# The place of GpSimd's shift in the combining of a Mamba and expert layer: behind the addition of the next group but one

## The chip, the cores and the metric

The kernel runs on one core of a Trainium2 chip. The metric is the time of one execution on the device, in microseconds; the median of three runs of the kernel before is 914.01 us.

## The reference

The input is 8 sequences of 1024 tokens of 128 numbers. A first block (a Mamba-2 mixer and a small MLP) gives x1. A second block routes each of the 8192 tokens to 2 of 8 experts (with a capacity), and adds the two gated results of a token to y. The last step, which is what the change touches, is a layer norm of y without weights and a residual:

```python
m = jnp.mean(x, axis=-1, keepdims=True)
v = jnp.var(x, axis=-1, keepdims=True)
return (x - m) / jnp.sqrt(v + eps)
...
x = x + _layernorm(_L0_ffn_ref(_layernorm(x, axis=-1), L0_ffn_Wr, ...), axis=-1)
```

All of it is float32.

## The kernel before, in words

The program goes through stages with a barrier of all engines between them. In the last one GpSimd gathers token rows for each expert by indirect DMA (L1809), TensorE runs the two matrix products, and GpSimd scatters the gated results into a DRAM buffer, `choice_rows` (L1817), which has one half for the first and one for the other expert of each token.

Then comes the combining. Its 64 tiles of 128 tokens are cut into 19 groups: 14 of four tiles, then groups of 2, 2, 2, 1 and 1 (L1717). For each group:

- SP loads both halves, `ys` and `yb` (L1792, L1793; a load of four tiles is 256 KB), and stores the result (L1797). The store of group n stands in its queue behind the loads of group n+8.
- GpSimd adds the halves: `both`, L1825, one tensor_tensor over 128x512.
- VectorE takes the statistics of each tile: `moments`, L1940, then `combined`, L1946, which makes mean and variance.
- ScalarE takes the root of the variance: `rooted`, L1899.
- VectorE makes the reciprocal: `inverse`, L1951.
- GpSimd negates the mean (`minus_mean`, L1829) and multiplies it with the reciprocal (`shift`, L1834), both over 128x4.
- ScalarE applies scale and shift to each tile: `normal`, L1905.
- VectorE adds x1: `add_x1`, L1955.

All of this lies in SBUF; in the trace `ys`, `yb` and `x1` all bear the name arena, the shift is c_shift, the reciprocal c_rs, the root c_sd, mean and variance c_mv.

Each engine runs its program in the order that `in_turn` (L1743) unrolls from a list of pairs of lag and step: in its round i an engine does, for each pair in the order of the list, the step of group i - lag. The lists are:

```python
in_turn(GROUPS, [(0, load), (8, store)])                                        # SP, L1798
in_turn(GROUPS, [(0, both), (1, minus_mean), (1, shift)])                       # GpSimd, L1835
in_turn(GROUPS, [(0, rooted), (1, normal)])                                     # ScalarE, L1907
in_turn(GROUPS, [(0, moments), (1, inverse), (0, combined), (2, add_x1)])       # VectorE, L1956
```

An engine does its instructions strictly in this order; `need(engine, semaphore, n)` waits until the step of group n that raises the semaphore is done. So on VectorE the reciprocal of group n comes behind the statistics of group n+1. The values that a group's small steps pass on (`c_mv`, `c_rs`, `c_sd`, `c_sh`, `c_nm`) have places of their own for every group; only the raw statistics, `c_st`, have two places in turn.

Of the kernel before, what the change touches and what calls it, by code (L numbers as in the profile page):

```python
# [58 lines left out]
def need(eng, sem, t, back=0):  # L59

    value = t + 1 - back
    if not isinstance(value, int) or value > 0:
        eng.wait_ge(sem, value)
# [33 lines left out]
def build(nc, x, ln_w, ln_b, in_proj_w, conv_w, conv_b, dt_bias, A_log, D_skip, rms_w, out_proj_w,  # L97
# [4 lines left out]
    with ExitStack() as ctx:  # L102
# [449 lines left out]
        with ExitStack() as st:  # L552
# [47 lines left out]
            def staged(stages):  # L600

                for i in range(PAIRS + max(lag for lag, _ in stages)):
                    for lag, stage in stages:
                        if 0 <= i - lag < PAIRS:
                            stage(i - lag)
# [475 lines left out]
        with ExitStack() as st:  # L1081
            st.callback(stage_over)
            NB, G = 4, 2
            GROUPS, N = TILES // G, G * P
# [602 lines left out]
        with ExitStack() as st:  # L1687
# [30 lines left out]
            GROUPS = len(widths)  # L1718
# [17 lines left out]
            def of_group(g):  # L1736
                return slice(first_tile[g], first_tile[g + 1])
# [5 lines left out]
            def in_turn(steps, stages):  # L1743

                for i in range(steps + max(lag for lag, _ in stages)):
                    for lag, stage in stages:
                        if 0 <= i - lag < steps:
                            stage(i - lag)
# [52 lines left out]
            @block.gpsimd  # L1801
            def _(g):
                def fetch(n):
                    need(g, s_pt, n, RING)
                    need(g, s_g1, n, RING)
                    need(g, s_g2, n, RING)
                    for i in range(sizes[n]):
                        c = starts[n] + i
                        g.indirect_dma_start(xg[:, n % RING, i, :], None, table,  # L1809
                                             bass.IndirectOffsetOnAxis(ap=token_of[:, c:c + 1], axis=0),  # L1810
                                             bounds_check=TOKENS - 1, oob_is_err=False).then_inc(s_xg[n % RING], 16)

                def leave(n):
                    need(g, s_yo, n)
                    for i in range(sizes[n]):
                        c = starts[n] + i
                        g.indirect_dma_start(choice, bass.IndirectOffsetOnAxis(ap=choice_of[:, c:c + 1], axis=0),  # L1817
                                             yo[:, n % RING, i, :], None, bounds_check=2 * TOKENS - 1,
                                             oob_is_err=False).then_inc(s_scat[n % RING], 16)
                g.wait_ge(filled, 16 * FILLS)  # L1820
                staged([(0, fetch), (LAG, leave)])

                def both(n):
                    g.wait_ge(s_in[n], 32)
                    g.tensor_tensor(ys[:, of_group(n)], ys[:, of_group(n)], yb[:, of_group(n)], ALU.add).then_inc(s_ys2, 1)  # L1825

                def minus_mean(n):
                    need(g, s_var, n)
                    g.tensor_scalar(c_nm[:, n, 0:widths[n]], c_mv[:, n, 0:widths[n], 0], -1.0, None, ALU.mult).then_inc(s_nm, 1)  # L1829

                def shift(n):
                    need(g, s_nm, n)
                    need(g, s_rs, n)
                    g.tensor_tensor(c_sh[:, n, 0:widths[n]], c_nm[:, n, 0:widths[n]], c_rs[:, n, 0:widths[n]], ALU.mult).then_inc(s_sh, 1)  # L1834
                in_turn(GROUPS, [(0, both), (1, minus_mean), (1, shift)])  # L1835

            @block.tensor
            def _(pe):
# [142 lines left out]
```

## Time and profile before

| | |
|---|---|
| median of 3 runs | 914.01 us (913.89 to 914.7) |
| the profiled execution | 914.42 us, its span 912.7 us |
| GpSimd busy over the span | 474.8 us (52%) |
| VectorE busy over the span | 602.5 us (66%) |
| ScalarE busy over the span | 493.2 us (54%) |
| TensorE matmuls busy over the span | 675.3 us (74%) |
| the combining's first load is issued at | 847.96 us |
| its first addition starts at | 851.52 us |
| the last addition of x1 starts at | 904.28 us |

The span runs from the first to the last instruction of the profiled execution; all times inside it count from its start. The whole program has stages with different limits, and the shares of the span say little of the last one; TensorE does nothing in the combining.

### The profile page before, as it was taken

How to read it: one execution, taken by the hardware profiler on the slowest of the kernel's cores; microseconds unless marked ns; L12 is line 12 of the kernel's file. 1: busy time of each engine (PE TensorE's matmuls, PEld its weight loads, DVE VectorE, ACT ScalarE, POOL GpSimd, SP SyncE). 2: the span in 40 equal slices, each digit the busy share in tenths (PEclk: the TensorE clock that was granted, in tenths of full speed). 3: DMA queues.
4: the chain of work that ended last, by engine and by line, in shares of the span. 5: the costliest groups of instructions: out<-in, count | busy, mean ns of one | idle time of the engine just before them, and what ended most of it. 6: DMA issues, size and time to landing. Idle time of an engine off the chain costs nothing. (4 is left out here: it accounts for less than half of the span.)

```text
span 912.7 us, 14173 instructions
## 1 busy us (share of the span) xinstructions
PE 675.3 (74%) x3646; PEld 480.7 (53%) x3646; DVE 602.5 (66%) x2110; ACT 493.2 (54%) x1207; POOL 474.8 (52%) x631
## 2 busy tenths in 40 slices
PE   7556999999999997999999702163896777976000
PEld 3224677777777775789999501132553444543000
DVE  7755999999999983799999687795221111111354
ACT  4764566666666665788886225252442333333254
POOL 7502576676667664234443230002677777776564
PEclk9876999999999998999999655555999999899555
DMA  8930000000000001500000021002222222211862
GB/s 212 394 115 1 1 1 1 1 1 2 1 1 2 1 1 42 144 1 2 2 0 1 1 113 76 0 0 62 45 74 74 72 74 71 74 50 42 280 202 78
DMA packets 50406, 52.84 MB, mean 58 GB/s; under 512 B 7576, under 2 KB 39624, under 8 KB 50080
## 3 DMA queue, kind: packets, MB, share of 16 engines
q1 hardware_dynamic: 44496, 41.62, 14.1%
q0 software_dynamic: 5120, 10.37, 4.3%
q8 instruction: 28, 0.46, 0.2%
q14 instruction: 42, 0.34, 0.1%
q10 hardware_dynamic: 720, 0.05, 0.1%
HBM read 28.04 MB, written 24.18 MB: 57 GB/s over the span
## 5 line engine op out<-in xcount | busy, mean ns | idle before, releaser
L836 DVE SCALAR_TENSOR_TENSOR s_cv<-s_pU,tap_w,s_cv 128x256 f32<-128x256 f32 x384 | 159.6, 477 | 20.0 <-ACT s_cv L769 19.5
L1809 POOL DMA_INDIRECT arena<-token_rows,token_of x80 | 81.1, 1014 | 118.3 <-issue 118.0
L1817 POOL DMA_INDIRECT choice_rows<-arena,choice_of x80 | 79.6, 995 | 31.1 <-issue 22.9
L1932 DVE TENSOR_TENSOR arena<-e_pB,e_gate 128x384 f32<-128x384 f32 (+2 forms) x24 | 14.5, 602 | 121.6 <-PE e_pB L1868 121.6
L1883 ACT ACTIVATE e_h<-e_pH,e_bcols 128x384 f32<-128x384 f32 (+2 forms) x96 | 58.6, 616 | 63.8 <-PE e_pH L1852 61.1
L642 POOL TENSOR_TENSOR s_xa<-s_xt,arena 128x512 f32<-128x512 f32 x32 | 34.4, 1075 | 103.1 <-ACT s_xt L787 103.1
L674 PE MATMUL s_pU<-arena,w_in 128*128 128x262 f32 x256 | 72.6, 408 | 11.5 <-DVE s_cv L836 8.1
L769 ACT ACTIVATE s_cv<-s_pU,tap_b,tap_w 128x256 f32<-128x256 f32 x128 | 65.7, 560 | 27.6 <-PE s_pU L674 27.0
L1852 PE MATMUL e_pH<-e_xgT,e_w 128*128 128x384 f32 (+2 forms) x192 | 79.0, 559 | 0.0
L1860 PE MATMUL e_pO<-e_h,e_w 128*128 128x384 f32 (+2 forms) x192 | 72.7, 522 | 0.4 <-ACT e_oT L1890 0.4
L1315 PE MATMUL m_pM<-w_m,m_h 128*128 128x128 f32 x512 | 62.5, 275 | 0.0
L1306 PE MATMUL m_pH<-m_hT,w_m 128*128 128x256 f32 x256 | 60.7, 380 | 2.1 <-ACT m_h L1189 1.5
L1315 PEld LDWEIGHTS m_pM<-w_m,m_h 128*128 128x128 f32 x512 | 59.7, 192 | 0.2 <-issue 0.2
L674 PEld LDWEIGHTS s_pU<-arena,w_in 128*128 128x128 f32 x256 | 45.4, 199 | 20.8 <-DVE s_cv L836 11.0
L1150 POOL TENSOR_TENSOR arena<-arena,m_un 128x256 f32<-128x256 f32 (+1 forms) x32 | 22.4, 701 | 64.9 <-DVE m_un L1225 64.9
L1860 PEld LDWEIGHTS e_pO<-e_h,e_w 128*128 128x128 f32 x192 | 36.5, 191 | 33.1 <-issue 20.3
L1852 PEld LDWEIGHTS e_pH<-e_xgT,e_w 128*128 128x128 f32 x192 | 38.2, 210 | 27.0 <-issue 18.8
L1306 PEld LDWEIGHTS m_pH<-m_hT,w_m 128*128 128x128 f32 x256 | 46.2, 190 | 7.5 <-ACT m_hT L1182 2.6
L1189 ACT ACTIVATE m_h<-m_pH,b_col 128x256 f32<-128x256 f32 x128 | 50.1, 484 | 0.0
L1924 DVE COPY e_xgT<-e_pT 128x384 f32<-128x384 f32 (+2 forms) x24 | 14.4, 599 | 48.6 <-PE e_pT L1843 48.6
L787 ACT ACTIVATE s_xt<-s_pTr 128x512 f32<-128x512 f32 x32 | 19.1, 597 | 47.7 <-PE s_pTr L684 47.7
L1890 ACT ACTIVATE e_oT<-e_pO,e_bcols 128x384 f32<-128x384 f32 (+2 forms) x24 | 14.8, 616 | 54.9 <-PE e_pO L1860 54.9
(289 smaller groups left out, 1873.8 us busy)
## 6 DMA issues: line engine op xcount, KB each, us to landing
choice_rows<-zrow SPq DMA_DIRECT2D x16, 512.0 KB, 6.9
arena<-choice_rows SPq DMA_DIRECT2D x28, 256.0 KB, 5.1
token_rows<-arena SPq DMA_DIRECT2D x8, 520.0 KB, 5.8
n_x<-in_L_attn_x_dram SPq DMA_DIRECT2D x8, 512.0 KB, 7.6
arena<-in_L_attn_x_dram SPq DMA_DIRECT2D x8, 512.0 KB, 4.7
e_w<-in_L_ffn_W_dram SPq DMA_DIRECT2D x16, 256.0 KB, 3.2
out_dram<-arena SPq DMA_DIRECT2D x14, 256.0 KB, 2.5
decay_rows<-arena SPq DMA_DIRECT2D x2, 1024.0 KB, 4.7
```

The costliest lines, as they stand in the source:

```text
L642: g.tensor_tensor(heads(xa[:, p % 3, :]), heads(xt[:, p % 2, :]), spread(pre, p), ALU.mult).then_inc(s_xa, 1)
L674: pe.matmul(pU[m % 2][:, 0:G2 * XBLK], w_in[:, P * m:P * (m + 1)], xT[:, G2 * p:G2 * (p + 1), :].rearrange("p t c -> p (t c)"), start=True ...
L769: a.activation(by_tile(cv[:, p % 2, m, :]), columns(m)[:, :, 0:P], ACT.Identity, bias=tap_b[:, m:m + 1], scale=tap_w[:, m, 0:1]).then_inc( ...
L836: v.scalar_tensor_tensor(out=by_tile(cv[:, p % 2, m, :]), in0=columns(m)[:, :, tap:tap + P], scalar=tap_w[:, m, tap:tap + 1], in1=by_tile( ...
L1189: ins = a.activation(h1[:, m % NB, c, :], pH[half_][:, N * (c % 2):N * (c % 2 + 1)], ACT.Relu, bias=b1_col[:, c:c + 1])
L1306: ins = pe.matmul(pH[half_][:, N * c:N * (c + 1)], w_m1[:, P * f:P * (f + 1)], hT[:, m % NB, :], start=True, stop=True)
L1315: ins = pe.matmul(pM[m % 2][:, P * i:P * (i + 1)], h1[:, m % NB, c, P * i:P * (i + 1)], w_m2[:, c, :], start=(c == 0), stop=(c == NF - 1))
L1809: g.indirect_dma_start(xg[:, n % RING, i, :], None, table, bass.IndirectOffsetOnAxis(ap=token_of[:, c:c + 1], axis=0), bounds_check=TOKENS ...
L1817: g.indirect_dma_start(choice, bass.IndirectOffsetOnAxis(ap=choice_of[:, c:c + 1], axis=0), yo[:, n % RING, i, :], None, bounds_check=2 * ...
L1852: pe.matmul(pH[c][:, 0:w], we1[:, expert(n) % 2, P * c:P * (c + 1)], xgT[:, n % 3, 0:w], start=True, stop=True).then_inc(s_ph, 1)
L1860: ins = pe.matmul(pO[:, 0:w], we2[:, expert(n) % 2, c, :], hb[:, n % 2, c, 0:w], start=(c == 0), stop=(c == NF - 1))
L1883: a.activation(hb[:, n % 2, c, 0:w], pH[c][:, 0:w], ACT.Silu, bias=bcols[:, f:f + 1]).then_inc(s_h, 1)
```

## The change

GpSimd's list gives the two small steps a lag of 2 in place of 1: in round i, behind the addition of group i, it makes the negated mean and the shift of group i - 2. The other engines' lists stay as they are.

```diff
-                in_turn(GROUPS, [(0, both), (1, minus_mean), (1, shift)])
+                in_turn(GROUPS, [(0, both), (2, minus_mean), (2, shift)])
```

At the start of the combining, in GpSimd's row (L1817 scatters the last results of the experts, L1825 is the addition):

```order
 L1809 DMA arena<-token_rows,token_of 128x130 x2
 L1817 DMA choice_rows<-arena,choice_of 16384x128 x20
-L1825 TENSOR_TENSOR arena<-arena 128x512 x2
-L1829 TENSOR_SCALAR c_minus<-c_mv 128x4
-L1834 TENSOR_TENSOR c_shift<-c_minus,c_rs 128x4
-L1825 TENSOR_TENSOR arena<-arena 128x512
+L1825 TENSOR_TENSOR arena<-arena 128x512 x3
 L1829 TENSOR_SCALAR c_minus<-c_mv 128x4
 L1834 TENSOR_TENSOR c_shift<-c_minus,c_rs 128x4
```

Three additions stand ahead of the first shift where there were two; from there on one addition and one pair follow each other as before, but the pair is that of a group earlier. At the end of GpSimd's row, where the groups are small:

```order
 L1834 TENSOR_TENSOR c_shift<-c_minus,c_rs 128x2
 L1825 TENSOR_TENSOR arena<-arena 128x128
+L1829 TENSOR_SCALAR c_minus<-c_mv 128x2
+L1834 TENSOR_TENSOR c_shift<-c_minus,c_rs 128x2
 L1829 TENSOR_SCALAR c_minus<-c_mv 128x1
 L1834 TENSOR_TENSOR c_shift<-c_minus,c_rs 128x1
```

The pair of the last group of two tiles used to come directly behind the addition of the first group of one tile; now it comes behind the last addition, and two pairs of one tile follow it. The rows of TensorE, VectorE, ScalarE and SP are the same.

## Rows read from the trace of the kernel before

**Rows 1.** The page: busy tenths of GpSimd and the DMA engines, 40 slices.

```profile
POOL 7502576676667664234443230002677777776564
...
DMA  8930000000000001500000021002222222211862
```

**Rows 2.** The chain of waits around 870 us (start us, us, what).

```profile
869.12 1.70 POOL arena L1825
...
870.91 0.87 DVE c_stats L1940 x4
...
872.01 0.20 POOL c_shift L1834
```

**Rows 3.** Timeline of GpSimd (start us, us, engine, line, operation, idle before).

```profile
854.65 1.26 POOL L1825 TENSOR_TENSOR arena<-arena 128x512 f32<-128x512 f32 x1 [1.88 <-DMA arena<-choice_rows]
855.88 0.23 POOL L1829 TENSOR_SCALAR c_minus<-c_mv 128x4 f32<-128x4 f32 x1
857.05 0.20 POOL L1834 TENSOR_TENSOR c_shift<-c_minus,c_rs 128x4 f32<-128x4 f32 x1 [0.94 <-DVE c_rs L1951]
857.20 1.26 POOL L1825 TENSOR_TENSOR arena<-arena 128x512 f32<-128x512 f32 x1
...
869.08 1.74 POOL L1825 TENSOR_TENSOR arena<-arena 128x512 f32<-128x512 f32 x1
870.78 0.21 POOL L1829 TENSOR_SCALAR c_minus<-c_mv 128x4 f32<-128x4 f32 x1
...
893.62 0.20 POOL L1834 TENSOR_TENSOR c_shift<-c_minus,c_rs 128x4 f32<-128x4 f32 x1 [1.02 <-DVE c_rs L1951]
...
903.22 0.20 POOL L1829 TENSOR_SCALAR c_minus<-c_mv 128x1 f32<-128x1 f32 x1
903.53 0.19 POOL L1834 TENSOR_TENSOR c_shift<-c_minus,c_rs 128x1 f32<-128x1 f32 x1
```

**Rows 4.** Timeline of VectorE, one round.

```profile
870.91 0.87 DVE L1940 BATCH_NORM_STATS2 c_stats<-arena 128x6 f32<-128x128 f32 x4 [1.22 <-POOL arena L1825]
871.70 0.16 DVE L1951 RECIPROCAL c_rs<-c_sd 128x4 f32<-128x4 f32 x1
...
872.12 0.66 DVE L1955 TENSOR_TENSOR arena<-arena 128x512 f32<-128x512 f32 x1
```

**Rows 5.** Waits, 855 to 904, then 893.5 to 904 us (us, times, longest).

```profile
POOL c_shift L1834 <- DVE c_rs L1951: 16.0, 18, 1.0
...
POOL c_shift L1834 <- DVE c_rs L1951: 3.9, 6, 1.0
```

**Rows 6.** Timelines of VectorE and GpSimd where their additions meet.

```profile
898.18 1.19 DVE L1955 TENSOR_TENSOR arena<-arena 128x512 f32<-128x512 f32 x1 [0.17 <-ACT arena L1905]
899.30 0.47 DVE L1940 BATCH_NORM_STATS2 c_stats<-arena 128x6 f32<-128x128 f32 x2
...
898.10 0.72 POOL L1825 TENSOR_TENSOR arena<-arena 128x256 f32<-128x256 f32 x1
...
9.65 1.47 POOL L295 TENSOR_TENSOR n_hn<-n_hc,n_scale 128x768 f32<-128x768 f32 x1 [0.15 <-DVE n_scale L488]
...
10.06 1.08 DVE L493 SCALAR_TENSOR_TENSOR n_shift<-moments,n_scale 128x8 f32<-128x8 f32 x1
```

**Rows 7.** Timeline of ScalarE, one round.

```profile
872.44 1.63 ACT L1905 ACTIVATE arena<-arena,c_shift,c_rs 128x128 f32<-128x128 f32 x4
```

**Rows 8.** Busy by stretch: PE, PEld, DVE, ACT, POOL, PEclk, DMA share, GB/s.

```profile
894.00:904.00 10.00, 0.00 (x0) 0.00 (x0) 6.75 (x29) 7.93 (x22) 6.69 (x17) 0.50 0.34 106
858.00:863.00 5.00, 0.00 (x0) 0.00 (x0) 3.21 (x20) 2.96 (x9) 2.97 (x7) 0.50 1.05 391
```

**Rows 9.** Timeline of SP's queue, and DMA issues of 846 to 913 us.

```profile
860.88 0.51 SPq L1792 DMA_DIRECT2D arena<-choice_rows  x1
...
arena<-choice_rows SPq DMA_DIRECT2D x28, 256.0 KB, 5.1
```

**Rows 10.** Timeline of VectorE, its last addition.

```profile
904.28 0.29 DVE L1955 TENSOR_TENSOR arena<-arena 128x128 f32<-128x128 f32 x1 [0.17 <-ACT arena L1905]
```

## The prediction

> **What bounds the kernel now.** The page's slices come first: in the last two and a half of the 40 (from about 850 us) GpSimd is busy for four to seven tenths, so it isn't full, and the DMA share is at its height only at the start of that stretch [rows 1]. The change lies there alone. The chain of waits of that stretch says what sets its pace: it goes round in a ring of addition (L1825, GpSimd), statistics (L1940, VectorE), shift (L1834, GpSimd), and again the addition [rows 2]. The ring's times, from the rows: an addition starts at 869.08, the statistics of its group at 870.91 (1.83 later), the reciprocal (L1951) behind them at 871.70 (0.79), the shift at 872.01 (0.31) [rows 2 to 4], and the next addition 0.15 after a shift (857.05 to 857.20) [rows 3]. Together 3.08 us a group. Nothing in it has to be a ring: the reciprocal belongs to group n, but VectorE reaches it only behind the statistics of group n+1, which want the addition of n+1; and the addition of n+2 stands on GpSimd behind the shift of n. GpSimd idles for it 16.0 us in 18 waits, always for L1951 [rows 5]. From the first shift (857.05) to the thirteenth (893.62) there are twelve such rounds, 36.57 us, 3.05 each [rows 3].
>
> The addition itself is priced in two ways: the second took 1.26 us, the seventh 1.74 [rows 3]. Ahead of the second VectorE had no addition of x1 (L1955) to make yet; in the even rounds one starts 0.42 after the reciprocal, at 872.12, some 0.04 before GpSimd's [rows 2 to 4]. The reverse is there too: where GpSimd's addition began first (898.10), VectorE's at 898.18 took 1.19 in place of 0.66 [rows 4, 6]. At the start of the program a VectorE operation on 8 columns took 1.08 us; it began 0.41 us into a 1.47 us multiplication on GpSimd and ended with it [rows 6]. So of two such operations the later one waits for the earlier to be over, and doesn't merely run slower.
>
> Here a rule of the Trainium skill differs: "Advanced Engine Details and Errata", section on VectorE's performance modes, names as the conflict with GpSimd only VectorE instructions in a two-port mode, and its table gives tensor_tensor no such mode. By that alone VectorE's addition would delay nobody, and the time would be that of the lower end of the first rival; the trace disagrees (1.19 against 0.66 us).
>
> **The change, part by part.** No instruction, DMA, buffer or semaphore is added or removed. Only GpSimd's row changes: each pair of L1829 and L1834 goes behind one more addition. SP's queue, VectorE's, ScalarE's rows are as before.
>
> 1. The ring goes. The addition of n+2 is no longer behind the shift of n, whose reciprocal by then has mostly been made. GpSimd alone would need 1.23 us (854.65 to 855.88) for the addition, 0.31 from L1829 to its L1834 (903.22 to 903.53) and 0.15 to the next: 1.69; with a wait of 0.48 (1.74 less 1.26) for VectorE's addition it is 2.17 a group [rows 3].
>
> 2. What is late next. The shift of n now comes behind the addition of n+2, so ScalarE's L1905 of group n comes then, and VectorE's L1955 of n (unchanged, behind the statistics of n+2) has to wait for it, and the statistics of n+3 stand behind that. This is a ring over two groups: shift of n to its L1905 0.43 (872.01 to 872.44), four activations 1.63 [rows 7], L1955 0.59 (1.12 from its start at 898.18 to the next instruction, less the 0.53 that it waited [rows 6]), statistics of n+3 0.79, reciprocal of n+2 to shift of n+2 0.31 [rows 2, 4]. Sum 3.75, or 1.88 a group. On top come the waits at the port. L1955 now starts when ScalarE is through, no longer just ahead of GpSimd's addition, and GpSimd runs ahead; so it is likely to find an addition begun. Behind one of half the size it waited 0.53, and a full one is 0.54 longer (1.26 less 0.72) [rows 3, 6]: up to 1.07. In a ring of two groups only the group that is on the ring pays; I take one full wait: 3.75 + 1.07 = 4.82, 2.41 a group. The bounds are no wait (then the 2.17 of point 1 decides) and a full wait of every kind (third and fourth rival).
>
> 3. The start. The shift of group 0 goes behind the addition of group 2, which must have landed. Its 512 KB land, at the 391 GB/s of the stretch 858 to 863, 1.3 us after those of group 1; rates just before are lower, so I take 1.5: 856.15. Then 1.23 and 0.31: the first shift is at 857.7, 0.6 later than before [rows 3, 8]. Bounds: 0 and 1.5.
>
> 4. Twelve rounds of 2.41 are 28.9 us; with 0.6, the thirteenth shift is reached 36.6 - 29.5 = 7.1 us earlier.
>
> 5. The tail. Behind the thirteenth shift come five small groups, in which GpSimd still waits 3.9 us in 6 waits for L1951, 1.0 of them before that shift: 2.9 [rows 5]. They go likewise, but ScalarE is busy 7.93 of the 10 us there, so at most 2.1 can be had [rows 8]. With the same port waits as above I take 1.5; bounds 0 and 2.1.
>
> 6. Transfers. A group moves two loads of 256 KB and a store of 256 KB, 786 KB. At 391 GB/s (DMA share 1.05) that is 2.0 us, under 2.41, so it isn't the bound [rows 8]. A load is issued behind the store nine groups before it (load 9 at 860.88) and takes 5.1 us; in seven rounds of 2.41 less the ring's latency some 11 us are there [rows 9]. Covered; without this cover the price would be 5.1 us once. The Trainium skill, "SBUF — State Buffer", gives about 358 GB/s for HBM to a NeuronCore; by it the transfers would want 2.2 us a group, an estimate which leaves the sum as it is. The row has 391.
>
> From the last L1955 (904.28) to the span's end at 912.7 are 8.4 us [rows 10], a store and the end of the program: unchanged.
>
> Sum: 7.1 + 1.5 = 8.6 us off. The profiled execution took 914.42 (span 912.7), so 905.8; it lies 0.41 above the median of the runs shown, 914.01, so the forecast is 905.4.
>
> **The rivals.**
>
> First, **the port hardly matters**: L1955 settles in the gap of GpSimd's L1829 and L1834 as it did before just ahead of the addition. For it: engines that wait for each other often fall into step, as in the twelve equal rounds. Against: GpSimd would be busy nearly throughout, so there are few gaps. Then 2.17 x 12 = 26.0; 36.6 - 26.6 = 10.0, tail 2.1: 12.1 off, 901.9. Its lower end is **no wait at the port at all**, a chance of its own of 0.03 within these, since rows 6 speak against it: the transfers' 2.0 a group are 24.0, the shifts give 12.0 and the tail 2.1, 899.9.
>
> Second, **it doesn't do what it says, since another wait takes the place at once**. VectorE's idle before the statistics is only moved. Then within 1.8 us of 914. Speaks against: the three engines each have less than 2.2 us of work per 3.05 us.
>
> Third, **a wait at the port for every group**, L1955 behind a full addition and the small operations of both groups of the ring behind an L1955, at most the 0.48 that an addition waits, for each: 3.75 + 1.07 + 0.9 = 5.7, 2.86 a group; 34.3 + 0.6, tail 0: 1.7 off; half of these 0.9 gives 2.64 a group, 31.7, and 4.3 off. About 911.
>
> Fourth, **slower: the shift gets stuck behind the addition two groups on**. GpSimd, running ahead, has just begun an addition when the reciprocal of n+2 comes ready, so the shift waits 1.23, and that addition has waited 0.48 for VectorE. The ring over two groups is then 3.75 + 1.07 + 1.71 = 6.53, 3.27 a group: 39.2 + 0.6 is 3.2 us more, 917.2. It decides from 6.0 us a ring ((36.57 - 0.6) / 6), that is, from 2.25 us of waits in it; I forecast 1.07. For it: GpSimd's work in order can't let a ready shift past. Against: L1829 of n waits for nothing late, and a GpSimd that runs ahead is stopped by L1834 waiting for L1951, which brings it back into step.
>
> **How the numbers follow.** Forecast 0.60 (903.5 to 908); first rival 0.22; third 0.09; second 0.04; fourth 0.05. 0.2% of 914 is 1.8 us, about what a measurement can tell from no change. Faster 0.91, same 0.04, slower 0.05. The range reaches down to the first rival with part of its lower end and up to the edge of the third: 900.5 to 910.0; outside it are the second, the fourth, most of the third and a little below, under 2 in 10. Both signs don't share the chance evenly, so no second range is needed.
>
> **What would show it.** In the profile after: additions L1825 of groups 2 to 4 start 1.7 us apart or as their loads land; later ones some 2.4 apart on average and not evenly; idle of L1834 for L1951 falls from 16.0 to under 5; some of VectorE's 128x512 L1955 take 1.2 to 1.7 us where nearly all took 0.66; the last L1955 is at about 896, and 8.4 us stay behind it. If rounds are 2.2 and L1955 stays at 0.66, the first rival; if rounds are over 3.05, the fourth. I am wrong about the ring if ScalarE's L1905 isn't what L1955 waits for. DMA share over 0.95 through to 885 with waits of L1825 for loads would make point 6 wrong.

## The result, and the profile after

The changed kernel takes 904.47 us in the median of 4 runs (904.27 to 905.34), against 914.1 of the kernel before, shared with these runs (913.89 to 914.7): a ratio of 0.9888, interval 0.9871 to 0.9905. In a second set of runs it was 905.41 against 914.27, ratio 0.9909 (0.9893 to 0.9924). So 8.9 to 9.6 us, about 1.0%, are gone. The profiled execution took 904.27 us, its span is 902.6. The forecast was 905.4, its range 900.5 to 910.0.

The page of the changed kernel, the lines that answer to [rows 1]:

```profile
span 902.6 us, 14173 instructions
...
POOL 7502576676676674234443340000767777776584
...
DMA  8930000000000000600000004000322222221493
```

A slice is 22.6 us. In the last but one, which the combining fills, GpSimd is busy for 8 tenths where it was for 6, and the DMA engines for 9.

The timeline of GpSimd, answering to [rows 3]; columns are start us, us, engine, line, operation, idle before:

```profile
853.72 2.53 POOL L1825 TENSOR_TENSOR arena<-arena 128x512 f32<-128x512 f32 x2 [2.16 <-DMA arena<-choice_rows]
...
856.53 0.20 POOL L1834 TENSOR_TENSOR c_shift<-c_minus,c_rs 128x4 f32<-128x4 f32 x1
...
865.67 1.26 POOL L1825 TENSOR_TENSOR arena<-arena 128x512 f32<-128x512 f32 x1
866.90 0.66 POOL L1829 TENSOR_SCALAR c_minus<-c_mv 128x4 f32<-128x4 f32 x1
868.49 0.20 POOL L1834 TENSOR_TENSOR c_shift<-c_minus,c_rs 128x4 f32<-128x4 f32 x1 [0.93 <-DVE c_rs L1951]
868.64 1.74 POOL L1825 TENSOR_TENSOR arena<-arena 128x512 f32<-128x512 f32 x1
...
870.65 0.68 POOL L1834 TENSOR_TENSOR c_shift<-c_minus,c_rs 128x4 f32<-128x4 f32 x1
871.29 1.26 POOL L1825 TENSOR_TENSOR arena<-arena 128x512 f32<-128x512 f32 x1
...
872.97 1.26 POOL L1825 TENSOR_TENSOR arena<-arena 128x512 f32<-128x512 f32 x1
...
884.86 0.20 POOL L1834 TENSOR_TENSOR c_shift<-c_minus,c_rs 128x4 f32<-128x4 f32 x1 [0.23 <-DVE c_rs L1951]
```

The third addition is no longer behind a shift: it directly follows the second (853.72, x2). The first shift is at 856.53, the thirteenth at 884.86: 28.33 us for the twelve rounds that took 36.57. The rounds aren't even. From 865.67 additions start at 868.64, 871.29 and 872.97: 2.97, 2.65, 1.68, and this pattern comes three times in a row from 858 us on. Three groups take 7.30 us, 2.43 each.

The timeline of VectorE, answering to [rows 4, 6, 10]:

```profile
865.75 1.74 DVE L1955 TENSOR_TENSOR arena<-arena 128x512 f32<-128x512 f32 x1 [0.57 <-ACT arena L1905]
867.41 0.86 DVE L1940 BATCH_NORM_STATS2 c_stats<-arena 128x6 f32<-128x128 f32 x4
...
868.60 0.66 DVE L1955 TENSOR_TENSOR arena<-arena 128x512 f32<-128x512 f32 x1
...
870.58 0.69 DVE L1955 TENSOR_TENSOR arena<-arena 128x512 f32<-128x512 f32 x1
...
873.05 1.73 DVE L1955 TENSOR_TENSOR arena<-arena 128x512 f32<-128x512 f32 x1 [0.58 <-ACT arena L1905]
...
894.13 0.29 DVE L1955 TENSOR_TENSOR arena<-arena 128x128 f32<-128x128 f32 x1 [0.61 <-ACT arena L1905]
```

The wait of a GpSimd and a VectorE operation for each other, as in [rows 6], is called the port below, as in the prediction. L1955 takes 1.74 us in every third group: it began at 865.75, 0.08 us behind GpSimd's addition of 865.67, and was let in when that was over. In the next group (868.60) VectorE was first, and GpSimd's addition took 1.74. In the third (870.58) VectorE was first again, and GpSimd's small shift took 0.68 in place of 0.20.

The waits from 847 to 903 us of the changed kernel, answering to [rows 5] (us in total, times, longest):

```profile
POOL arena L1825 <- DMA arena<-choice_rows: 6.9, 2, 4.8
POOL c_shift L1834 <- DVE c_rs L1951: 5.9, 9, 0.9
DVE arena L1955 <- ACT arena L1905: 4.3, 7, 0.8
ACT arena L1905 <- POOL c_shift L1834: 2.2, 4, 0.6
```

The 16.0 us that L1834 waited are 5.9. The 4.3 us in which L1955 waits for ScalarE were 0.2 in the same window of the kernel before, and the 2.2 in which ScalarE waits for a shift were 0.3. VectorE's waits before the statistics (L1940 for L1825), without the long one for the stage's first addition, fell from 19.3 us to 2.2.

What sets the pace can be read in the chain of waits of one such pattern (start us, us, what):

```profile
865.75 0.03 DVE arena L1955
865.78 1.62 issue
867.41 0.86 DVE c_stats L1940 x4
...
868.49 0.20 POOL c_shift L1834
868.69 1.48 POOL arena L1825
...
870.65 0.69 POOL c_shift L1834
...
871.37 1.66 ACT arena L1905 x4
...
873.05 0.04 DVE arena L1955
```

From the L1955 of group 3 (865.75) to that of group 6 (873.05): 1.66 until the next statistics, since L1955 is held at the port; 0.78 to the reciprocal, 0.30 to the shift of group 5 (868.49). From there two ways lead on, and they end 0.07 us apart. The chain shows GpSimd's: its addition of 868.64 is held up by 0.48, and GpSimd comes to the shift of group 6 at 870.65. The other is ScalarE's: L1905 of group 5 starts 0.43 behind the shift of group 5 and takes 1.63, and its end lets L1955 of group 5 start at 870.58. That is 4.83 us for two groups. The third costs less: the L1955 at 870.58 holds back the shift of group 6, which has come to 870.65, by 0.48; then L1905 (871.37, 1.66) and the L1955 of group 6. 2.47 us. Together 7.30. By GpSimd's way three waits at the port lie in these 7.30: 1.08, 0.48 and 0.48.

Not all of the profile's 10.15 us (914.42 less 904.27) belong to the change. The first load is issued at 846.80 in it and at 847.96 in the kernel before, though nothing ahead of it is different. And what comes before the second addition is up to the loads: in the kernel before it starts 6.69 us behind the first load, here 6.92. So below each kernel is also read **from the second addition to the end of the span**, which leaves out what ran earlier and the waits for the first two groups' loads: 58.05 us before (854.65 to 912.7), 48.88 after (853.72 to 902.6), a difference of 9.17.

### The profile page after: what moved, and what is told of

It is laid out like the page before. It is cut to its first block and busy times, and to the rows that moved or that the text cites. A ratio compares the mean times of both kernels' runs of the same rounds, so it can differ in the third digit from the quotient of the medians.

```text
span 902.6 us, 14173 instructions
## 1 busy us (share of the span) xinstructions
PE 674.2 (75%) x3646; PEld 480.2 (53%) x3646; DVE 606.2 (67%) x2110; ACT 492.3 (55%) x1207; POOL 475.0 (53%) x631
## 5 line engine op out<-in xcount | busy, mean ns | idle before, releaser
L1817 POOL DMA_INDIRECT choice_rows<-arena,choice_of x80 | 79.6, 995 | 31.0 <-issue 22.6
L1852 PE MATMUL e_pH<-e_xgT,e_w 128*128 128x384 f32 (+2 forms) x192 | 81.2, 572 | 0.0
```

What stands on the lines that cost most here:

```text
L1852: pe.matmul(pH[c][:, 0:w], we1[:, expert(n) % 2, P * c:P * (c + 1)], xgT[:, n % 3, 0:w], start=True, stop=True).then_inc(s_ph, 1)
```

## The experiments

Each kernel's reading of that stretch, worked out from two rows of its own trace, beside the medians:

| kernel | pair lag, L1955 lag | 2nd addition to end, us | 1st to 13th shift, us | median, us | ratio to before |
|---|---|---|---|---|---|
| before | 1, 2 | 58.05 | 36.57 | 914.1 | |
| before, again | 1, 2 | 57.98 | 36.55 | 914.56 (one run) | |
| changed | 2, 2 | 48.88 | 28.33 | 904.47 | 0.9888 (0.9871 to 0.9905) |
| changed, again | 2, 2 | 48.88 | 28.30 | 905.41 | 0.9909 (0.9893 to 0.9924) |
| only the shift moved | 1 and 2, 2 | 52.52 | 31.54 | 908.57 | 0.9922 (0.9893 to 0.9951) |
| pair at lag 3 | 3, 2 | 49.70 | 27.77 | 907.7 | 0.9913 (0.9881 to 0.9945) |
| L1955 at lag 3 | 2, 3 | 43.97 | 24.08 | 901.07 | 0.9841 (0.9814 to 0.9867) |
| before, L1955 at lag 3 | 1, 3 | 57.95 | 36.09 | 914.15 | 0.9987 (0.997 to 1.0004) |
| before, L1955 with one SBUF input | 1, 2 | 51.46 | 31.41 | 906.9 | 0.992 (0.9899 to 0.994) |
| changed, L1955 with one SBUF input | 2, 2 | 43.02 | 22.76 | 901.3 | 0.9868 (0.9823 to 0.9913) |
| best order | 2 and 1, 3 | 42.66 | 23.04 | 899.48 | 0.9838 (0.9816 to 0.9861) |
| best order, again | 2 and 1, 3 | 42.52 | 22.91 | 898.57 | 0.9829 (0.9816 to 0.9842) |

The medians come from several sets of runs, whose kernel before lies at 914.1 to 915.1; the stretch repeats within 0.15 us in the three kernels that were profiled twice. I go by it for differences of a few tenths. Each kernel's saving by its median, against the kernel before of its own set of runs, is within 1 us of its saving by the stretch, but for the changed kernel with one SBUF input: 12.9 us by the medians, 15.0 by the stretch.

**Only the shift moved.**

```diff
-                in_turn(GROUPS, [(0, both), (2, minus_mean), (2, shift)])
+                in_turn(GROUPS, [(0, both), (1, minus_mean), (2, shift)])
```

> GpSimd keeps minus_mean (L1829) at lag 1 and only the shift (L1834) goes to lag 2. My theory: what the change took away is the wait of the shift for the reciprocal behind the next statistics, but L1829 of group n-1 waits for L1946 of n-1, so GpSimd is kept within one group of VectorE; it gives most of the gain, about 2.7 us less than the changed kernel: 907.2 us. Rival A (only the shift's place counts): the same as the changed kernel, 904.5. Rival B (L1829's own wait was as costly as the shift's): near before, over 911.

Measured: 52.52, that is 3.64 longer than the changed kernel and 5.53 shorter than before. Neither rival holds. Its waits from 855 to 900 us:

```profile
POOL c_minus L1829 <- DVE c_mv L1946: 14.1, 9, 1.8
DVE arena L1955 <- ACT arena L1905: 7.4, 10, 1.3
```

The shift's wait is all but gone, but L1829 now waits 14.1 us for the mean, up to 1.8 at a time. The timelines of GpSimd and VectorE where it does:

```profile
868.78 0.57 POOL L1829 TENSOR_SCALAR c_minus<-c_mv 128x4 f32<-128x4 f32 x1 [1.84 <-DVE c_mv L1946]
869.31 0.19 POOL L1834 TENSOR_TENSOR c_shift<-c_minus,c_rs 128x4 f32<-128x4 f32 x1
...
868.20 0.15 DVE L1951 RECIPROCAL c_rs<-c_sd 128x4 f32<-128x4 f32 x1
...
868.60 0.66 DVE L1955 TENSOR_TENSOR arena<-arena 128x512 f32<-128x512 f32 x1
```

The negated mean needs nothing but the mean, and still it had to move with the shift. At lag 1 it stands ahead of the shift of the group before and wants VectorE's L1946, which comes behind the reciprocal that this shift wants; by then L1955 (868.60) has begun, and L1829 takes 0.57 in place of 0.22. So the shift starts 1.11 us behind its reciprocal (868.20 to 869.31), where the changed kernel has 0.30. The ring of two groups, from the L1955 of 865.87 to that of 871.22, takes 5.35 us, 2.67 a group. My price was 2.7 us of time for 3.64 measured; the direction and the place were right.

**The addition of x1 a group later.** The changed kernel, with VectorE's list ending in lag 3:

```diff
-                in_turn(GROUPS, [(0, moments), (1, inverse), (0, combined), (2, add_x1)])
+                in_turn(GROUPS, [(0, moments), (1, inverse), (0, combined), (3, add_x1)])
```

> The changed kernel, with VectorE's addition of x1 (L1955) at lag 3 in place of 2. Theory: in the changed kernel rounds are set by a ring through shift, L1905, L1955 (which waits for ScalarE 4.3 us and at the port) and the statistics; with L1955 a group later it never waits for ScalarE, rounds fall from 2.43 to about 2.17 (GpSimd's own work and one wait at the port), 4.8 us less than the changed kernel: 899.7 us. Rival (GpSimd's work and the port set the rounds in the changed kernel already, and L1955's wait for ScalarE is slack): within 1 us of 904.5, or slower by up to 1 us since the last additions come later.

Measured: 43.97, 4.91 less than the changed kernel (4.8 expected). Its waits, and its L1955:

```profile
POOL c_shift L1834 <- DVE c_rs L1951: 1.3, 3, 0.6
DVE arena L1955 <- ACT arena L1905: 0.4, 1, 0.4
```

```profile
872.70 1.01 DVE L1955 TENSOR_TENSOR arena<-arena 128x512 f32<-128x512 f32 x1
...
874.82 1.01 DVE L1955 TENSOR_TENSOR arena<-arena 128x512 f32<-128x512 f32 x1
```

L1955 waits for ScalarE once, 0.4 us, and takes 0.93 to 1.01 us in the first ten groups: it meets the tail of an addition and not a whole one. A round in the middle is 2.12 us (872.70 to 874.82), where I had expected 2.17; over all twelve it is 2.01. This settles what set the changed kernel's pace: the L1955 that waits for ScalarE, and what stands behind it. GpSimd was not full there; here it is, its round of 2.12 being the 1.69 of its own work and 0.44 by which L1829 is held up (0.66 in place of 0.22).

**The same in the kernel before.** The same edit of VectorE's list, with GpSimd's pair at lag 1.

> The kernel before (pair at lag 1) with L1955 at lag 3. Theory: the ring of before runs over addition, statistics, reciprocal, shift and holds no L1955, so nothing changes: 913.8 us, within 0.5. Rival (the gain of the run with L1955 later comes by itself and doesn't need the shift moved): about 909 us.

Measured: 57.95 against 58.05. The wait that sets its pace stands as it did, to be compared with [rows 5]:

```profile
POOL c_shift L1834 <- DVE c_rs L1951: 16.1, 18, 1.0
```

The second ring exists only once the first is gone. The step that is worth 4.9 us on top of the change is worth 0.1 without it.

**The pair at lag 3.**

```diff
-                in_turn(GROUPS, [(0, both), (2, minus_mean), (2, shift)])
+                in_turn(GROUPS, [(0, both), (3, minus_mean), (3, shift)])
```

> GpSimd's pair at lag 3, all else as in the changed kernel. Theory: nothing is left to gain from lag 2 to 3, the first shift comes one addition later and the ring over ScalarE and L1955 stays: 0.9 us slower than the changed kernel, 905.3 us. Rival (the reciprocal's wait, still 5.9 us in 9 waits, is on the path): up to 5 us faster, 900. Rival (a shift stuck behind a further addition delays L1955): 908 or more.

Measured: 49.70, 0.82 more than the changed kernel (0.9 expected).

```profile
POOL c_shift L1834 <- DVE c_rs L1951: 7.0, 10, 1.1
DVE arena L1955 <- ACT arena L1905: 5.6, 7, 2.1
```

L1834 still waits 7.0 us, so the 5.9 of the changed kernel weren't a wait that moving it further away could cure: VectorE is late there, not GpSimd early. The medians are of little help here (907.7 where before was 915.08, and the changed kernel in its own set 904.47 where before was 914.1); the sign rests on the stretch.

**The port, measured by itself.** L1955 adds what lies in a PSUM bank in place of x1, so that the addition of x1 is left out; the instruction keeps its size, its place and its waits, and has one SBUF input in place of two. Once in the kernel before, once in the changed one:

```diff
-                    v.tensor_tensor(ys[:, of_group(g)], ys[:, of_group(g)], x1[:, of_group(g), :], ALU.add).then_inc(s_ot, 1)
+                    v.tensor_tensor(ys[:, of_group(g)], ys[:, of_group(g)], pB[:, 0:P * widths[g]].rearrange("p (i d) -> p i d", d=D), ALU.add).then_inc(s_ot, 1)
```

> The kernel before, but L1955 adds what lies in the PSUM bank pB in place of x1 from SBUF: the addition of x1 is left out, the instruction keeps its size and place and has one SBUF input. Theory (a VectorE instruction with two SBUF inputs and a GpSimd one shut each other out): GpSimd's 128x512 additions all take 1.26 us in place of 1.74, rounds fall from 3.09 to 2.6, 6.8 us less than before: 907.3 us. Rival (the 0.48 us come from DMA traffic or from SBUF in general, not from that input): additions stay at 1.74 and the time at 914.

Measured: 51.46, 6.59 less than before (6.8 expected). The timelines of GpSimd and VectorE in one round of it:

```profile
871.41 0.20 POOL L1834 TENSOR_TENSOR c_shift<-c_minus,c_rs 128x4 f32<-128x4 f32 x1 [1.01 <-DVE c_rs L1951]
871.56 1.26 POOL L1825 TENSOR_TENSOR arena<-arena 128x512 f32<-128x512 f32 x1
...
871.51 0.65 DVE L1955 TENSOR_TENSOR arena<-arena,e_pB 128x512 f32<-128x512 f32 x1
...
872.93 0.87 DVE L1940 BATCH_NORM_STATS2 c_stats<-arena 128x6 f32<-128x128 f32 x4 [0.76 <-POOL arena L1825]
```

The same overlap as in [rows 3, 4]: L1955 at 871.51, GpSimd's addition at 871.56. It takes 1.26 us where the one at 869.08 took 1.74, and the statistics follow 1.37 after its start and not 1.83. DMA traffic was no less (a share of 0.92 from 870 to 880 us, 0.71 in the kernel before), so the rival falls: the 0.48 come with VectorE's second SBUF input.

> The changed kernel with the same replacement in L1955 (x1 is left out). Theory: no L1955 takes over 0.75 us and no small GpSimd operation 0.66; the ring over ScalarE is 3.8 us per two groups and transfers set 2.0 us a group; 6.2 us less than the changed kernel: 898.3 us. Rival (the port costs nothing there, since one ring only hides another): within 1 us of 904.5.

Measured: 43.02, 5.86 less than the changed kernel (6.2 expected). GpSimd and VectorE where the overlaps were, and the stretch 870 to 880 (busy by engine, clock, DMA share, GB/s):

```profile
871.90 1.27 POOL L1825 TENSOR_TENSOR arena<-arena 128x512 f32<-128x512 f32 x1
...
872.07 0.69 DVE L1955 TENSOR_TENSOR arena<-arena,e_pB 128x512 f32<-128x512 f32 x1
```

```profile
870.00:880.00 10.00, 0.00 (x0) 0.00 (x0) 9.60 (x54) 9.45 (x28) 8.69 (x17) 0.50 1.10 375
```

L1955 at 872.07 runs inside an addition of GpSimd (871.90 to 873.17) in 0.69 us; in the changed kernel that was 1.74. Rounds are 1.90 us. At 375 GB/s a group's 786 KB take 2.10 us, more than a round; the loads issued ahead allow that, and behind the first two additions L1825 waits for loads only twice more, 0.4 and 0.5 us. So the transfers aren't the bound yet, but close to it.

**A better order.** L1955 at lag 3, and GpSimd makes the shift of i-2 ahead of the negated mean of i-1:

```diff
-                in_turn(GROUPS, [(0, both), (2, minus_mean), (2, shift)])
+                in_turn(GROUPS, [(0, both), (2, shift), (1, minus_mean)])
...
-                in_turn(GROUPS, [(0, moments), (1, inverse), (0, combined), (2, add_x1)])
+                in_turn(GROUPS, [(0, moments), (1, inverse), (0, combined), (3, add_x1)])
```

> L1955 at lag 3 and on GpSimd the order addition of i, shift of i-2, negated mean of i-1: the shift no longer stands right behind its own negated mean (0.31 us from one to the other). Theory: GpSimd's round loses some 0.15 us, 2.0 to 2.1 us, 7 us less than the changed kernel and 2 less than with L1955 at lag 3 alone: 897.5 us. Rival (the negated mean at lag 1 ties GpSimd to VectorE, as in the run with only the shift moved): over 900, no better than L1955 at lag 3 alone.

Measured: 42.66, 6.22 less than the changed kernel (7 expected) and 1.31 less than with L1955 at lag 3 alone (2 expected). Here the negated mean at lag 1 is harmless. It stands behind the shift and finds its mean ready, so it delays no shift as it did in the run with only the shift moved; no run isolates this, since L1955's lag differs too:

```profile
873.07 0.64 POOL L1834 TENSOR_TENSOR c_shift<-c_minus,c_rs 128x4 f32<-128x4 f32 x1
873.68 0.21 POOL L1829 TENSOR_SCALAR c_minus<-c_mv 128x4 f32<-128x4 f32 x1
873.87 1.26 POOL L1825 TENSOR_TENSOR arena<-arena 128x512 f32<-128x512 f32 x1
```

```profile
872.75 0.91 DVE L1955 TENSOR_TENSOR arena<-arena 128x512 f32<-128x512 f32 x1
...
874.77 0.90 DVE L1955 TENSOR_TENSOR arena<-arena 128x512 f32<-128x512 f32 x1
```

```profile
870.00:880.00 10.00, 0.00 (x0) 0.00 (x0) 10.00 (x51) 9.08 (x26) 10.00 (x16) 0.50 1.07 350
```

GpSimd, and VectorE, are busy for 10.00 us of 10, the time in which they hold each other up counted in (L1955 0.90 in place of 0.66, the shift 0.64 in place of 0.20). From 865 to 880 us only ScalarE still waits, for shifts, 0.2 us at most. A round in the middle is 2.02 us, 0.10 less than with L1955 at lag 3 alone.

**Again, for the scatter.**

> The changed kernel once more, for one question: in the first profiled pair the combining began 1.16 us earlier with the change (its first load at 846.80 against 847.96), though nothing ahead of it was changed. Theory: that part of the difference is scatter of what runs before; the stretch from the first load to the end of the span is 55.8 us again within 0.5, and the start lies anywhere from 846 to 853. Rival: the change moves the start too; then it is again near 846.8 and before's near 848.

> The kernel before once more, one profile. Theory: first load to end 64.7 us within 0.5, start anywhere from 846 to 853. Rival: start at 848.0.

> The best order so far (addition of i, shift of i-2, negated mean of i-1, and L1955 at lag 3) against before in more rounds: first load to end 48.6 us within 0.5, 16.1 less than before; ratio 0.983 to 0.984.

The first load of the changed kernel, and that of the kernel before, in the timelines of SP's queue:

```profile
849.05 0.33 SPq L1792 DMA_DIRECT2D arena<-choice_rows  x1
```

```profile
847.98 0.33 SPq L1792 DMA_DIRECT2D arena<-choice_rows  x1
```

The changed kernel's is at 849.05 this time, 2.25 later than in its first profile; over all kernels here it lies between 846.80 and 852.25. The kernel before is at 847.98, as the rival said, but one more profile of it can't tell a fixed start from scatter. The changed kernel's two starts, one 1.16 us before and one 1.07 us behind that of the kernel before, can: the change doesn't move the start, and the 1.16 us of the first pair are scatter of what runs ahead. From first load to end the changed kernel took 54.75 us, not 55.8: 1.05 less, outside the 0.5 that I allowed, and all of it ahead of the second addition, which came 5.87 us behind the first load and not 6.92. From that addition on both profiles read 48.88. The kernel before took 64.82, within its 0.5. The best order is at 0.9829, 49.11 us from the first load, 15.7 less than before: both just outside what I had named (48.6 within 0.5, 0.983 to 0.984).

## Why the prediction was right

Range, sign and size held: 9.63 us between the medians, of which 9.17 in the combining, for a forecast of 8.6. By its points:

1. **The ring goes**: right. The third addition starts right behind the second, and GpSimd's 1.69 us round is there in one of three (871.29 to 872.97 is 1.68).

2. **What is late next**: the mechanism was right, the ring was drawn over too few groups. I had one full port wait in a ring of two groups, 4.82 us, 2.41 a group. Measured is a ring of three: two groups at 4.83 with that full wait (1.74 less 0.66 is 1.08, for my 1.07), then one at 2.47 with a wait of 0.48 for a small operation. The chain also has the 0.48 by which an addition is held up, on GpSimd's way through the same ring. I had held such waits for possible (third rival) and hadn't put them in the forecast. That 7.30 / 3 is 2.43 beside my 2.41 is in part luck: the two groups' 4.83 were right by their own terms, but that the third would come to half of them I hadn't worked out. By GpSimd's way the three groups have 2.04 us of waits at the port, 0.68 a group for my 0.54, and 5.26 of all else, 1.75 a group for my 1.88: two misses that cancel. Over the twelve rounds, with a quicker beginning, it is 2.36. The part of the ring without the port was priced well: 3.75 us for two groups, and the changed kernel with one SBUF input in L1955 has 3.79 (872.07 to the L1955 of 875.86).

3. **The start**: 0.6 later was forecast, since the third addition would have to wait for its loads. It didn't wait. Counted from the first load the first shift came 0.64 later (9.73 for 9.09), but that is luck: in the second profiles it came 0.53 earlier (8.70 for 9.23), as the loads scatter. Counted from the second addition it is 0.41 and 0.44 later (2.81 and 2.83 for 2.40 and 2.39), the price of one more addition ahead of it less the wait for L1951 that is gone.

4. **Twelve rounds**: 28.9 us forecast, 28.33 measured. With the start, 7.83 us (38.97 less 31.14, each from the second addition to the thirteenth shift) for 7.1.

5. **The tail**: 1.5 forecast; thirteenth shift to last L1955 was 10.66 and is 9.27: 1.39.

6. **Transfers**: covered, as stated. L1825 waits for loads twice, 6.9 us in all, and both waits are the first two additions. The sign of trouble that I had named, a DMA share over 0.95 through to 885 together with such waits, didn't come: the share is 0.96 from 867 to 880 us and 0.55 from 880 to 885, and no later addition waits for a load.

The signs named beforehand: the 1.74 us of some L1955 came as told; the idle of L1834 came to 5.9, not under 5; the last L1955 is at 894.13, which with 1.16 us of scatter ahead of it is 895.3 beside the forecast 896.

The rivals: the port mattered (the run without its second SBUF input was 5.86 us quicker), so the first falls; no full new wait took the place at once (VectorE's waits before the statistics fell from 19.3 us to 2.2), so the second does; the third came in part, with 0.96 of small waits in three groups for its 0.9 in two, and the full wait once in three groups and not in two; the fourth, the shift stuck behind a further addition, would show as ScalarE waiting for L1834, which is 2.2 us in 4 times and at most 0.6. The prediction set against its forecast what the Trainium skill says in "Advanced Engine Details and Errata", section on VectorE's performance modes, which names two-port modes as a conflict. That section is silent on VectorE instructions with two SBUF inputs, and doesn't say that there is no other conflict, so the prediction read more into it than it states. Taken as the whole rule it doesn't fit: fp32 tensor_tensor from two SBUF tensors holds GpSimd up by 0.48 and is held up by 1.08, and with one SBUF input by neither. The Trainium skill's "SBUF — State Buffer", section "Who interferes with whom", does name VectorE instructions with two SBUF inputs against GpSimd ones that read SBUF, and calls the contention an exclusive lock; the two traces agree with that (GpSimd's addition 1.74 us against 1.26 with one input, L1955 1.74 against 0.69).

## What to carry to other kernels

When engines run their steps in a fixed order, follow the idle time round until it closes, and note for how many groups: a step's lag is worth moving only where it is in the ring that closes first, and the next ring can be priced from the same rows before anything is run (here the two groups came out at 4.83 for 4.82; how many groups the ring has was missed). Move all steps that tie the two engines, not only the one that waits (the negated mean cost 3.6 us of the gain when it stayed ahead of the shift; behind the shift, and with L1955 a group later, it did no harm at lag 1), and ask which step must then move on the other engine (L1955: 4.9 us here, 0.1 without the change). To read a change of a stage, measure from an instruction that the change can't touch; here that repeats within 0.15 us where whole runs scatter by 1 and more.

## What the runs showed of the hardware that I had not expected

- A GpSimd operation with one SBUF input of 4 columns (L1829) is held up by VectorE's two-input addition too: 0.66 us in place of 0.22 (866.90, beside the L1955 that starts once the addition of 865.67 is over).
- Waiting at the port makes the instruction itself look longer (1.74, 0.68); it shows in no list of waits. Of the changed kernel's loss to it, 5.86 us, only the durations tell.
- Issue times of one and the same program part scatter by up to 5.5 us between profiles (first load at 846.80 to 852.25), and the time from the first load to the second addition by 1.1 (5.87 to 6.92 in two profiles of the changed kernel). What makes them scatter wasn't looked into.
